# Where the next pair's first norm stands in a hand-written order of one core's work

## The reference, cut to what matters

```python
h = tokens(x)                       # 65 tokens: class token and 64 patches, times pos_embed
h = concatenate([h, txt], axis=1)   # 193 x 128
h = h + attn(layernorm(h))          # 8 heads, relative positions, group norms
h = h + ffn(layernorm(h))           # 8 experts, 512 wide, top-2 weights of a gate

def attn(x):
    qkv = group_norm(x @ W_qkv)     # over tokens and 8 channels
    logits = q k + q rpe_k + k rpe_q
    a = softmax(logits)
    return group_norm(a v + a rpe_v)

def ffn(x):
    top_p = top2(softmax(x @ Wg)), made to sum to 1
    return sum_i sum_e gelu(x * top_p[i] @ W1[e] + b1[e]) @ W2[e] + b2
```

## Time and profile before

| | us |
|---|---|
| median of 3 runs | 3425.13 |
| the three runs | 3424.44 to 3427.97 |
| the profiled execution's own time | 3423.42 |
| its span, first to last instruction | 3421.6 |

### The profile page before, as it was taken

The page is one execution under the profiler, slowest core; times in us unless marked ns, Lnnn a source line. Parts: engine busy times, 40 slices in busy tenths (PEclk is TensorE's granted clock), DMA queues, the critical chain, the costliest instruction groups (busy, mean ns, idle before and its releaser), DMA issues.

```text
span 3421.6 us, 65186 instructions
## 1 busy us (share of the span) xinstructions
PE 3200.4 (94%) x21952; PEld 2602.3 (76%) x21952; DVE 1981.0 (58%) x4052; ACT 1832.8 (54%) x3570; POOL 1447.1 (42%) x1350
## 2 busy tenths in 40 slices
PE   7977999999999999999999999999999999999998
PEld 5867777777777777777777777777777777777776
DVE  4644655566565556665555566655555666655554
ACT  4632555555555555555555555555555555555556
POOL 1010444455434444554444445544444555344446
PEclk9987999999999999999999999999999999999999
DMA  9961001111110011111101111111011111100110
GB/s 202 219 179 30 14 16 26 24 26 26 26 24 9 22 24 26 26 26 26 24 7 24 24 26 26 26 26 24 5 26 24 26 26 26 26 23 6 24 25 5
DMA packets 92174, 121.41 MB, mean 35 GB/s; under 512 B 8414, under 2 KB 86558, under 8 KB 87710
## 3 DMA queue, kind: packets, MB, share of 16 engines
q1 hardware_dynamic: 87714, 118.24, 14.9%
q10 hardware_dynamic: 4432, 2.79, 0.3%
HBM read 106.04 MB, written 14.97 MB: 35 GB/s over the span
## 4 chain that ended last, share of the span: by engine, by line
issue 39%; PE 25%; POOL 15%; DVE 9%; ACT 4%; DMA 0%; DVEq 0%; POOLq 0%; ACTq 0%; SPq 0%
POOL gelu L889 10%; PE bank L420 7%; POOL q_bd L918 4%; PE bank L461 4%; PE bank L429 3%; DVE gelu L607 3%; PE bank L433 2%; DVE dl L760 2%; PE bank L430 2%; ACT gelu L817 2%; DVE gst L650 1%; PE bank L493 1%; POOL rs L902 1%; ACT e L840 1%; PE bank L449 1%
## 5 line engine op out<-in xcount | busy, mean ns | idle before, releaser
L889 POOL TENSOR_TENSOR gelu<-gelu 128x386 f32<-128x386 f32 x1024 | 1068.3, 1055 | 1477.9 <-ACT gelu L818 1474.7
L817 ACT ACTIVATE gelu<-bank,b_s 128x386 f32<-128x386 f32 x1024 | 595.2, 581 | 878.2 <-DVE gelu L607 867.0
L420 PE MATMUL bank<-gelu,w_s 128*128 128x386 f32 x2048 | 834.8, 494 | 45.6 <-POOL gelu L889 41.4
L607 DVE TENSOR_TENSOR gelu<-bank,ratio 128x386 f32<-128x386 f32 x1024 | 565.1, 557 | 476.4 <-PE bank L433 470.7
L818 ACT ACTIVATE gelu<-gelu,b_s 128x386 f32<-128x386 f32 x1024 | 624.3, 610 | 0.0
L429 PE MATMUL bank<-x_hi,w_hi 128*128 128x386 f32 x1024 | 524.6, 512 | 78.0 <-ACT gelu L817 73.8
L420 PEld LDWEIGHTS bank<-gelu,w_s 128*128 128x128 f32 x2048 | 361.6, 189 | 105.6 <-POOL gelu L889 87.0
L517 PE MATMUL bank<-k_f,q_bd 128*128 128x193 f32 x1600 | 393.6, 328 | 8.2 <-DVE a_bd L700 8.2
L518 PE MATMUL bank<-rw,a_bd 128*128 128x193 f32 x1600 | 393.2, 328 | 0.0
L858 ACT ACTIVATE lp<-bank,mx 128x193 f32<-128x193 f32 x800 | 288.0, 419 | 195.5 <-DVE mx L710 194.3
L429 PEld LDWEIGHTS bank<-x_hi,w_hi 128*128 128x128 f32 x1024 | 193.9, 189 | 253.7 <-ACT gelu L817 176.6
(11 more groups left out here) (131 smaller groups left out, 4266.6 us busy)
## 6 DMA issues: line engine op xcount, KB each, us to landing
a_rep<-u_scratch SPq DMA_DIRECT2D x32, 1600.0 KB, 9.8
xt<-in_x SPq DMA_DIRECT2D x192, 196.0 KB
txt_s<-in_txt SPq DMA_DIRECT2D x32, 128.0 KB, 2.2
u_scratch<-k_f SPq DMA_DIRECT2D x32, 100.0 KB, 2.2
u_scratch<-q_f SPq DMA_DIRECT2D x32, 100.0 KB, 2.2
out<-o_s SPq DMA_DIRECT2D x64, 48.5 KB
out<-o_s SPq DMA_DIRECT2D x64, 48.0 KB
rv<-in_rel_v SPq DMA_DIRECT2D x1, 2624.0 KB, 14.0
```

Source lines behind the costliest of these rows:

```text
L420: mm(yb[:, 0:T2], w2_s[:, f, :], gelu1[:, f % RING, :], start=(f == 0), stop=(f == NF - 1)).then_inc(S["w2_done"], 1)
L607: v.tensor_tensor(gelu2[:, f % RING, :], zb[f % 2][:, 0:T2], ratio[:, :], ALU.mult).then_inc(S["z2_done"], 1)
L817: a(gelu1[:, f % RING, :], zb[f % 2][:, 0:T2], ACT.Gelu, bias=b1_s[:, f:f + 1]).then_inc(S["g_done"], 1)
L889: g.tensor_tensor(gelu1[:, f % RING, :], gelu1[:, f % RING, :], gelu2[:, f % RING, :], ALU.add).then_inc(S["hs_done"], 1)
```

## The change

Only the string `SCHEDULE` changes. The steps `txt`, `mean1`, `var1` and `bc1` of pair n+2 move from behind `place0` to places among `log7` to `tr1`. `proj` stands behind `rel6`; `gmean`, `gvar` and `gaff` stand around `pv1`, `place0` and `place1`. One FFN step (`c`) moves from ahead of `am0` to between `place0` and `place1` or behind; between `ovar` and `oaff`, and between `var2` and `bc2`, there are now two. The number of each step is the same.

```diff
--- before.py
+++ after.py
@@ -82,10 +82,10 @@
 EARLY = "txt mean1 var1 bc1 proj gmean gvar gaff".split()
 OUTPUT = "w2t ot otr ocopy".split()
 SCHEDULE = (
-    "c c c c am0 c qs0 c c vt hkeep log0 am1 log1 qs1 log2 am2 log3 qs2 log4 log5 am3 log6 qs3 log7 log8 "
-    "qs4 log9 log10 log11 log12 tr0 tr1 rel0 c tr2 rel1 c tr3 rel2 tr4 rel3 tr5 rel4 tr6 rel5 rel6 "
-    "c pv0 c rec0 pv1 c rec1 place0 txt place1 c c omean mean1 c ovar c var1 oaff c bc1 oh2 c proj mean2 c "
-    "gmean c var2 gvar c bc2 c gaff c gate c c gate2 c c c c bcast w2t xin w2t w2t ot a otr a ocopy hres a"
+    "c c c am0 c qs0 c c vt hkeep log0 am1 log1 qs1 log2 am2 log3 qs2 log4 log5 am3 log6 qs3 log7 txt log8 "
+    "qs4 log9 mean1 log10 log11 var1 log12 tr0 tr1 bc1 rel0 c tr2 rel1 c tr3 rel2 tr4 rel3 tr5 rel4 tr6 rel5 rel6 "
+    "proj c pv0 c rec0 gmean pv1 c rec1 gvar place0 c place1 gaff c c omean c ovar c c oaff c oh2 c mean2 c var2 c c "
+    "bc2 c gate c c gate2 c c c c bcast w2t xin w2t w2t ot a otr a ocopy hres a"
 ).split()
 AHEAD = SCHEDULE.count("a")
```

## The result

The changed kernel takes 3484.36 us (median of 4 runs, 3481.72 to 3488.14), the kernel before 3425.51 beside it: a ratio of 1.0172, 95% interval 1.0156 to 1.0189. It is slower, by 1.7%. The profiled execution took 3488.14 us; its span is 3486.3.

A forecast was written before the change was run, and what follows sets the result against it. TensorE, busy 94%, sets the pace. The short turn's 93.61 plus 5.16, -0.4, -0.4, -0.2, +2.2 and +0.3 gives 100.3 us a turn against 98.05; thirty turns +67, opening -3, plus 1.7 to the median: 3489 us, range 3415 to 3535.

The forecast's parts named there:

- the short turn: The one turn without the steps of the pair after next: 93.61 us in the kernel before, the forecast's starting point.
- The gelu behind `gaff`: FFN step after `omean`: TensorE waits for gelu behind `gaff`'s activations, 1.3 to 2.2 us; +2.2 us a turn taken.
- The wait at `mean2`: Second norm's chain: `oaff` makes `mean2` late for want of FFN steps between; the short turn's 1.27 us kept whole.
- The wait behind `ovar`: Between `ovar` and `oaff`: the extra FFN step takes some 0.2 us off the short turn's wait.
- The 5.16 us added to the short turn: TensorE work a full turn has beyond the short turn, added to 93.61 to give 98.77 us.
- The sum behind `var2`: `var2`, one step behind `mean2`: +0.3 us a turn, bounds 0 and 0.9, the upper with a sum held behind the power.
- The gate: Gate's matmuls to `bcast`: 8.99 us as in the short turn, against 10.34 in a full turn; L760 about 0.4 us.
- The rival in which its long wait stays: L760 at the gate still falls in the second sum: 1.35 us a turn stay, 3529 us; chance 0.18.
- Transposes and `place1`: Wait for exponentials at the transposes shrinks, -0.4 us a turn; a step before `place1` covers the reciprocal, -0.4 us.
- The opening: Opening turn, without FFN work: the first norm is hidden under the logits, about -3 us once, bounds 0 and -8.
- The free passage: Rival: no row of sums meets `gaff` and `oaff`; 98.0 us a turn, some 3421 us, no change; chance 0.11.
- the hidden chains: Rival: `gaff`'s and `oaff`'s activations end in time, both waits nought; 96.7 a turn, 3381 us; hidden or partly hidden 0.15.

The follow-up runs named there:

- Experiment 1: `gaff` one FFN step later, on the changed kernel: 3409.8 us, 0.9959 of the kernel before.
- experiment 4: Mean, scale and one product of the group norms' small instructions put in PSUM, on the changed kernel: 3425.52 us, 1.0005 of the kernel before.
- experiment 2: `oaff` one FFN step earlier, on the changed kernel: 3497.47 us, 1.0216 of the kernel before.
- Experiment 3: The gate's addition (L760) written to PSUM and read there by the reciprocal, on the kernel before: 3385.06 us, 0.9890.
- Experiment 5: Only `txt`, `mean1`, `var1` and `bc1` moved among logits and transposes, on the kernel before: 3429.01 us, 1.0012.
- experiment 6: Both PSUM edits (gate's addition and group norms' small products) on the kernel before: 3402.16 us, 0.9937.
- experiment 8: Both PSUM edits plus `txt`, `mean1`, `var1` and `bc1` moved among logits and transposes, on the kernel before: 3387.88 us, 0.9895.
- 7: Both PSUM edits on the changed kernel with `gaff` one FFN step later: 3409.17 us, 0.9956 of the kernel before.

## Why the prediction was right

It said 3489 us and the change takes 3484; the profiled execution was to be 3487.4 and was 3488.1. Turn by turn the working held too, 100.3 against 99.98 (100.41 every third), but some of its terms were off and cancelled. That the profiled execution came within 1 us is luck: the turns at the full clock were charged 10 us too much in all, and this was made up by the clock (4.5 us), the later patch embedding (4.0), an opening that gained less than charged (2) and the short turn (0.3). Against the median the forecast is 5 us high.

*The gelu behind `gaff`: right in place and size.* Charged 2.2 us; measured 1609.26 to 1611.40 start to start, less the 0.14 of `omean`: 2.0. The route is the one given: VectorE's part took 1.30 us (1607.82 to 1609.12) where 1.4 was taken, nearly all of it one instruction in one sum. Experiment 1 shows that this place sets the wait; experiment 4 splits it into 0.8 for SBUF and 1.1 for the four activations.

*The wait at `mean2`: right in size, wrong in its reason.* The short turn's 1.27 came back as 1.07. It does come from `oaff`, but the count of FFN steps between `oaff` and `mean2` as cover fell: with one more step there (experiment 2) the wait came back as 1.34 us at the FFN step just ahead of `mean2`, and the kernel got slower. The cost is VectorE's standing still through sums (experiment 4), and a part of it came from `gaff`'s wait ahead of it (experiment 1), so the two terms that were added up aren't independent. Removing the first alone gave back 2.3 us a turn, more than its own 2.0.

*The wait behind `ovar`: not as charged.* It was to lose 0.2 us; TensorE waits 0.21 us at 1614.98, as it waits 0.22 at this place of the short turn. From `omean` to `mean2` it still takes 0.5 us less than there, once the step added and `gaff`'s wait are taken off (6.89 against 7.37), 0.2 of it at `mean2`.

*The 5.16 us added to the short turn: 0.3 too much.* They are busy time, and matmuls overlap; start to start, the moved matmuls take 4.8.

*The sum behind `var2`: the most mis-sized term.* Charged 0.3 with an upper bound of 0.9; TensorE waits 0.52 us at 1624.66, and from `mean2` to the gate it takes 0.8 more than the short turn (8.17 against 8.57 less the one step that it has more). The upper bound was the right mechanism: a sum held behind the power.

*The gate: right.* 1627.49 to 1636.48 is 8.99 us, the short turn's figure, and L760 took 0.46 us. The rival in which its long wait stays fell. Experiment 3 adds what the wait was worth to the kernel before: 39 us. The change thus gave back 1.35 us a turn here and still lost, since the rest of the turn grew by 3.3 us (99.98 - 98.05 + 1.35).

*Transposes and `place1`: right.* From the first transpose to the step behind the sixteenth TensorE takes 2.31 us (1571.32 to 1573.63) against 2.75, which is the 0.4 charged; the wait for the exponentials is gone. `place1` doesn't wait in the full turns, which gave 0.3 start to start. Experiment 5 shows that in the kernel before the first of these brings nothing without the second; on experiment 6 it gave 14 us even so (experiment 8).

*The opening: sign right, size off.* -3 was charged, -1.0 came. In it the new order waits 3.03 us at `mean2`, the longest of those waits in the view above; before, with `mean1`, `var1`, `bc1` and the projection between, TensorE didn't wait there (the 1.3 in the view is the short turn's). The hidden chain gained, the uncovered one took back.

*The free passage and the hidden chains* both fell: the waits they needed gone are there, 1.07 and 1.85 us. By the Trainium skill (SBUF — State Buffer, Who interferes with whom) a VectorE instruction with two SBUF inputs waits for a running GpSimd instruction that reads SBUF, and one in a mode that uses both ports waits for any. Experiments 3 and 4 agree that the operands' place decides (2362 to 155 ns for L760, 884 to 170 for L652 on 128x4). That L760, with one SBUF input, ran in such a mode no run here shows, and why it sat through more than one sum (2362 ns on average) stays open.

*Not foreseen: the clock.* 0.45 us in every third turn, 10 times, some 4.5 us (last section).

## What to carry to other kernels

Price a moved chain by what it leaves as well: the steps on both sides of the hole lose their cover, and a wait put into the FFN stretch makes the sums behind it come in rows, in which the next small VectorE instructions stand. Before moving steps, look for small VectorE instructions whose length is many times their work beside a busy GpSimd; an output in PSUM freed the gate's (-1.1%), while the same cure where other work is late brought nothing. Take one wait away at a time and read what is late next: in experiment 6 the gain passed to another sum, in 7 it never came.

## What the hardware showed

TensorE's granted clock halves behind the long wait, in every third turn. Two stretches of 5 us at the same place of two turns, and a W2 product behind the wait in each (at the full clock and at half):

```profile
1611.00:1616.00 5.00, 4.39 (x19) 3.27 (x20) 2.43 (x6) 4.59 (x10) 3.77 (x5) 1.00 0.59 149
1711.00:1716.00 5.00, 4.63 (x14) 3.53 (x15) 1.28 (x3) 3.60 (x8) 3.26 (x4) 0.66 0.62 154
```

```profile
1612.03 0.81 PE L420 MATMUL bank<-gelu,w_s 128*128 128x386 f32 x2
```

```profile
1711.37 0.45 PE L429 MATMUL bank<-x_hi,w_hi 128*128 128x386 f32 x1 [1.86 <-ACT gelu L817]
...
1712.00 1.25 PE L420 MATMUL bank<-gelu,w_s 128*128 128x386 f32 x2
...
1719.74 0.92 PE L449 MATMUL bank<-h,con 128*128 128x386 f32 x2 [0.34 <-DVE h L750]
```

In both turns TensorE stood for 1.85 us just before; in one it then runs some 3.4 us at 1.2 GHz in place of 2.4 (worked out from the 0.66). That costs 1.7 us of work but only 0.45 us of the turn, since `mean2`'s wait shrinks from 1.07 to 0.34 us in its shadow. In experiment 2, with the same wait of 1.85, this happens in most turns (0.979 over the run against 0.990 in the kernel before). In the kernels whose longest wait is 1.1 us or less no full turn shows it. A wait on TensorE can so cost more than its length. Why one turn in three is hit, and not each, stays open.

The second is how far a small instruction's length depends on its phase to the sums: the same L652 on 128x4 takes 162 ns in the kernel before and 884 in the changed one, and L650 the other way (1563 and 137), with no change to either.
